# A graph convolution on one core: self loops' one-hot matrix on ScalarE, and the last four blocks prepared early and finished in a new order

## The reference

```python
h = jnp.maximum(_layernorm(x, axis=-1), 0.0)
# RGCN with mean over the neighbours of each type
out = h @ W_root + bias
for r in range(8):
    m = (edge_type == r)
    msg = h[src] @ W[r] * m[:, None]
    agg = segment_sum(msg, dst, num_segments=n)
    cnt = segment_sum(m, dst, num_segments=n)
    out = out + agg / maximum(cnt, 1.0)[:, None]
return x + out
```

## Time and profile before

| | |
|---|---|
| median of 3 runs | 1065.55 us (1061.63 to 1066.65) |
| profiled execution, its own time | 1065.97 us |
| its span, first to last instruction | 1064.2 us |
| POOL busy | 774.6 us (73%) |
| DVE busy | 800.8 us (75%) |
| PE busy | 784.8 us (74%) |
| PEld busy | 610.3 us (57%) |
| ACT busy | 273.8 us (26%) |
| mean granted TensorE clock | 0.783 of full speed |

### The profile page before, as it was taken

The page is one execution under the profiler, slowest core; times in us unless marked ns, Lnnn a source line. Parts: engine busy times, 40 slices in busy tenths (PEclk is TensorE's granted clock), DMA queues, the critical chain, the costliest instruction groups (busy, mean ns, idle before and its releaser), DMA issues.

```text
span 1064.2 us, 19429 instructions
## 1 busy us (share of the span) xinstructions
PE 784.8 (74%) x4294; PEld 610.3 (57%) x4294; DVE 800.8 (75%) x2602; ACT 273.8 (26%) x672; POOL 774.6 (73%) x821
## 2 busy tenths in 40 slices
PE   0377777777778787877878778787777877778756
PEld 0256666556566565665656556565565655656545
DVE  8799999878887766867767676776767767767674
ACT  5632222222222222222222222222222222222200
POOL 7677777777777777777777777777777777777730
PEclk9988797887877877687787877878777787777865
DMA  8594222212222222222222222222222222222210
GB/s 261 159 228 95 55 55 58 54 54 57 55 57 56 56 57 54 56 54 54 56 54 57 54 55 56 54 56 54 56 55 53 56 55 57 55 54 56 54 34 6
DMA packets 51561, 70.85 MB, mean 67 GB/s; under 512 B 13843, under 2 KB 36662, under 8 KB 51526
## 3 DMA queue, kind: packets, MB, share of 16 engines
q0 software_dynamic: 25632, 52.55, 18.9%
q1 hardware_dynamic: 25894, 17.90, 6.4%
HBM read 63.99 MB, written 6.40 MB: 66 GB/s over the span
## 4 chain that ended last, share of the span: by engine, by line
issue 37%; POOL 35%; DVE 10%; PE 7%; DMA 4%; ACT 1%; SPq 1%; POOLq 0%; DVEq 0%; ACTq 0%
POOL hg L498 35%; PE acc L1458 4%; DMA hg<-h_table,idx 4%; PE fin L1491 2%; DVE onehot L1021 2%; DVE ring L1037 2%; DVE fin L1073 1%; DVE x_all L1121 1%; DVE blk L1079 1%; DVE loophot L1026 1%; PE acc L1462 1%; SPq L402 1%; DMA x_all<-in_x 1%; PE acc L1465 0%; PE zp L1480 0%
## 5 line engine op out<-in xcount | busy, mean ns | idle before, releaser
L498 POOL DMA_INDIRECT hg<-h_table,idx x741 | 712.1, 961 | 225.8 <-issue 219.7
L1458 PE MATMUL acc<-onehot,hg 128*128 128x104 f32 (+2 forms) x1602 | 486.9, 406 | 205.0 <-DMA hg<-h_table,idx 180.3
L1458 PEld LDWEIGHTS acc<-onehot,hg 128*128 128x128 f32 x1602 | 314.5, 244 | 323.5 <-issue 202.3
L1021 DVE TENSOR_SCALAR onehot<-iota,key_f 128x104 f32<-128x104 f32 (+2 forms) x801 | 234.1, 311 | 32.2 <-DVE ring L1037 17.0
L1462 PE MATMUL acc<-onehot,ones_bf 128*128 128x104 bf16 (+2 forms) x801 | 221.9, 277 | 0.0
L610 ACT ACTIVATE idx<-src_i 128x3 int32 (+1 forms) x247 | 50.7, 205 | 542.0 <-PE acc L1465 542.0
L1037 DVE TENSOR_TENSOR ring<-ring,acc 128x512 f32 x267 | 179.9, 674 | 2.7 <-PE acc L1465 2.6
L1491 PE MATMUL fin<-w_sb,blk 128*116 128x128 f32 x864 | 159.2, 332 | 0.0
L1121 DVE SCALAR_TENSOR_TENSOR x_all<-fin,inv,x_all 116x128 f32 (+1 forms) x400 | 137.0, 342 | 15.9 <-PE fin L1491 15.4
L1491 PEld LDWEIGHTS fin<-w_sb,blk 128*116 128x116 f32 x864 | 144.6, 236 | 1.1 <-issue 0.5
L1073 DVE SCALAR_TENSOR_TENSOR fin<-ring,zp 128x464 f32<-128x464 f32 x108 | 69.6, 645 | 83.9 <-PE zp L1473 77.5
(11 more groups left out here) (135 smaller groups left out, 390.5 us busy)
## 6 DMA issues: line engine op xcount, KB each, us to landing
hg<-h_table,idx POOLq DMA_INDIRECT x741, 2.5
out<-x_all SPq DMA_DIRECT2D x53, 58.0 KB
x_all<-in_x SPq DMA_DIRECT2D x7, 384.0 KB, 6.5
h_table<-h_all SPq DMA_DIRECT2D x7, 384.0 KB
h_all<-h_table SPq DMA_DIRECT2D x5, 504.0 KB
x_all<-in_x SPq DMA_DIRECT2D x5, 504.0 KB
hg<-h_table,src_i POOLq DMA_INDIRECT x36, 5.3
w_sb<-in_L_gnn_W SPq DMA_DIRECT2D x1, 512.0 KB
```

What stands on the lines that cost most here:

```text
L498: nc.gpsimd.indirect_dma_start(out=hg[:, j, :], out_offset=None, in_=table, in_offset=bass.IndirectOffsetOnAxis(ap=idx[:, j:j + 1], axis=0 ...
L1021: nc.vector.tensor_scalar(onehot[:, t, 0:(e - a) * R].rearrange("p (r n) -> p r n", r=R), by_node[:, :, a:e], key_f[:, bass.ds(i * IT + t, ...
L1458: nc.tensor.matmul(both[:, 0, :, a:e], hg[:, slot, :], hot.rearrange("p (r n) -> p r n", r=R), start=(j == 0), stop=(j == n - 1), skip_gro ...
```

## The change

1. The comparison for `loophot` leaves VectorE. ScalarE makes the same matrix in two activations: the distance |iota - loop_key| into a new tile `loop_far`, then relu(1 - distance) into `loophot`. In iteration i and group q it does so for the following group, behind the index copy.
2. In iteration 15 TensorE transposes the own rows of blocks 50 to 53 straight from `h_all` into a free accumulator and ScalarE copies them to `tail_hT`; in iteration 16 TensorE makes their four root products with bias and VectorE adds them to `x_all` in one instruction.
3. In `end()` the four last blocks are made with a new `make_last_block`, which reads the own rows from `tail_hT` in SBUF and writes its intermediate to PSUM; the counts are transposed straight from the ring and their inverses computed from PSUM, for blocks 50 and 51 together; the products of a half start when that half of the block is there; root products, own rows and count copies are gone from there. The order of sums, blocks, additions and ring additions is new.
4. SyncE reads the flag before it waits for the stores.

```diff
                 stage(EARLY - 1, GROUPS - 1, GROUPS)
-                own(ENDB)
+                loop_onehot(EARLY + 1, 1)
                 stage(EARLY, 0, GROUPS)
-                take_counts(ENDB, slot_of(ENDB))
+                loop_onehot(EARLY + 2, 2)
                 stage(EARLY + 1, 1, GROUPS)
-                own_to_sbuf(ENDB)
-                counts_to_sbuf(ENDB)
-                for b in LASTB:
-                    own(b)
-                    own_to_sbuf(b)
-                    take_counts(b, slot_of(b))
-                    counts_to_sbuf(b)
...
+            def loop_onehot(g, q, wait_for=None):
...
+                nc.scalar.activation(loop_far[:, :], iota[0:GT * SLOTS, :], ACT.Abs,
+                                     bias=loop_key[:, bass.ds(g, 1)], scale=-1.0).then_inc(loop_far_ready, 1)
+                act.wait_ge(loop_far_ready, g + 1)
+                settled(act)
+                nc.scalar.activation(loophot[:, q, :], loop_far[:, :], ACT.Relu,
+                                     bias=ones[0:GT * SLOTS, 0:1], scale=-1.0).then_inc(loophot_ready, 1)
...
-                nc.vector.tensor_scalar(loophot[:, q, :], iota[0:GT * SLOTS, :], loop_key[:, bass.ds(g, 1)], None,
-                                        ALU.is_equal).then_inc(loophot_ready, 1)
...
+            def make_last_block(b):
...
+                for half, z_done in ((0, z_low), (1, z_high)):
+                    rs = slice(half * (R // 2), (half + 1) * (R // 2))
+                    dve.wait_ge(blk_made, 2 * b + half)
+                    nc.vector.scalar_tensor_tensor(out=tail_own, in0=ring[:, 1, rs, slot], scalar=LOOP_FLAG / 2, in1=h_b,
+                                                   op0=ALU.is_ge, op1=ALU.mult).then_inc(own_part_made, 1)
+                    dve.wait_ge(z_done, b)
+                    dve.wait_ge(own_part_made, 2 * b + half + 1)
+                    nc.vector.tensor_tensor(blk[:, rs, :], ring[:, 0, rs, slot], tail_own, ALU.add).then_inc(blk_made, 1)
...
             def end():   # VectorE
+                b0, b1, b2, b3 = TAILB
+                onehots(ENDI, 0, GT, inverse_counts(b0 - 1))
                 add_group(EARLY - 2, 3, at[0])
+                onehots(ENDI, 1, GT, add_terms(b0 - 1, range(0, 3)))
                 add_group(EARLY - 1, 4, at[1])
+                finish_sums(b0, EARLY)
                 finish_sums(b1, EARLY)
+                in_turn(add_terms(b0 - 1, range(3, ADDS)))
+                make_last_block(b0)
+                add_group(EARLY, 0, at[2], 2 * b0)
+                onehots(ENDI, 2, GT, [])
+                last_inverses(0, b0, 2)
+                add_last_terms(b0)
+                onehots(ENDI, 3, GT, [])
+                make_last_block(b1)
                 add_group(EARLY + 1, 1, at[3])
+                add_last_terms(b1)
+                onehots(ENDI, 4, GT, [])
+                add_group(EARLY + 2, 2, at[4])
...
                 add_group(EARLY + 4, 4, at_last[1])
                 finish_sums(b2, ENDG)
+                make_last_block(b2)
                 add_group(ENDG, 0, at_last[2])
+                last_inverses(1, b2, 1)
                 add_last_terms(b2)
                 add_group(ENDG + 1, 1, at_last[3])
                 finish_sums(b3, GALL)
+                make_last_block(b3)
+                last_inverses(2, b3, 1)
                 add_last_terms(b3)
...
             def end():   # TensorE
+                b0, b1, b2, b3 = TAILB
+                relations(b0 - 1, R // 2 - 1, R // 2, z_low)
+                root_of(b0 - 1)
+                relations(b0 - 1, R // 2, R, z_high)
                 sums_of(ENDI, 0, GT)
+                tail_counts(0, b0, 2)
+                last_relations(b0)
                 sums_of(ENDI, 1, GT)
                 sums_of(ENDI, 2, GT)
+                last_relations(b1)
                 sums_of(ENDI, 3, GT)
+                pe.wait_ge(tail_inv_step, 2)
                 sums_of(ENDI, 4, GT)
...
                 sums_of(ITERS - 1, 0, GT)
+                tail_counts(1, b2, 1)
+                last_relations(b2)
                 sums_of(ITERS - 1, 1, GT)
+                tail_counts(2, b3, 1)
+                last_relations(b3)
...
-            sp.wait_ge(stored, 16 * BLOCKS)
             sp.wait_ge(flag_ready, 1)
             general = sp.value_load(flag[0:1, 0:1], min_val=0, max_val=1)
+            sp.wait_ge(stored, 16 * BLOCKS)
```

More of the change, by code:

```diff
@@ L26 @@
 ENDG = (ITERS - 1) * GROUPS
-LASTB = range(BLOCKS - LAG - 1, BLOCKS)
-ENDB = LASTB[0] - 1
+TAILB = range(BLOCKS - LAG - 2, BLOCKS)
+ENDB = TAILB[0]
 ENDI = ITERS - 2
@@ L176, in rgcn @@
         hT = sb("hT", [P, BLK])
+        tail_hT = sb("tail_hT", [P, len(TAILB), BLK])
+        tail_unflag = sb("tail_unflag", [BLK, len(TAILB), R])
+        tail_cnt1 = sb("tail_cnt1", [BLK, len(TAILB), R])
+        tail_inv = sb("tail_inv", [BLK, len(TAILB), R])
         even = sb("even", [BLK, F])
@@ L672, in iteration @@
                         act.wait_ge(zeros_made, 1)
-                    g = g - 1
-                    if not isinstance(g, int) or (AHEAD - 1) * GROUPS <= g < GALL - GROUPS:
-                        stage(g, (q - 1) % GROUPS, GROUPS)
-                    elif (AHEAD - 3) * GROUPS <= g < (AHEAD - 2) * GROUPS:
-                        stage(g, (q - 1) % GROUPS, 2 * GROUPS)
+                    if not isinstance(g, int) or (AHEAD - 1) * GROUPS <= g - 1 < GALL - GROUPS:
+                        stage(g - 1, (q - 1) % GROUPS, GROUPS)
+                    elif (AHEAD - 3) * GROUPS <= g - 1 < (AHEAD - 2) * GROUPS:
+                        stage(g - 1, (q - 1) % GROUPS, 2 * GROUPS)
+                    if static(g):
+                        loop_onehot(g, q, 1)
+                    part_wait = PART_GROUPS.index(g + 1) + 1 if isinstance(g, int) and g + 1 in PART_GROUPS else None
+                    loop_onehot(g + 1, (q + 1) % GROUPS, part_wait)
                     if b is not None:
@@ L690, in iteration @@
                         words_to_sbuf(part_at(i, q, 3, 2))
+                    if static(i, STATICS - 2) and q == 2:
+                        act.wait_ge(tail_T, 1)
+                        nc.scalar.activation(tail_hT[:, :, :].rearrange("p b n -> p (b n)"), tailT,
+                                             ACT.Copy).then_inc(tail_hT_ready, 1)
                     if part_at(i, q, 3, 4) is not None:
@@ L1252, in whole_order, with add_tail_roots @@
                 nc.vector.tensor_reduce(bad1[:, :], bad[:, :], AX.X, ALU.max).then_inc(bad_ready, 1)
+            def add_tail_roots():
+                x_tail = x_all[0:BLK, TAILB[0]:, :].rearrange("p b f -> p (b f)")
+                dve.wait_ge(tail_root, 1)
+                nc.vector.tensor_tensor(x_tail, tail_roots, x_tail, ALU.add).then_inc(tail_root_added, 1)
             def parts_ready():
@@ L1483, in relations @@
             def relations(b, r0, r1, done):
-                if r0 == 0:
+                if r0 == 0 and done is None:
                     pe.wait_ge(blk_made, 2 * b + 2)
@@ L1512, in iteration @@
                         pe.wait_ge(loop_key_ready, part_at(i, q, 4, 0) + 1)
+                    if static(i, STATICS - 2) and q == 3:
+                        pe.wait_ge(tail_hT_ready, 1)
+                    if static(i, STATICS - 1) and q == 3:
+                        pe.wait_ge(tail_root_added, 1)
                     if n:
@@ L1531, in iteration @@
                             relations(b, 0, R // 2 - 1, None)
+                    if static(i, STATICS - 2) and q == 1:
+                        tail_transposes()
+                    if static(i, STATICS - 1) and q == 1:
+                        tail_products()
                     if part_at(i, q, 3, 1) is not None:
@@ L1540, in check_sum, with tail_transposes, tail_products @@
                 pe.wait_ge(loop_key_ready, len(PARTS))
+            def tail_transposes():
+                pe.wait_ge(group_added, (STATICS - 2) * GROUPS - 1)
+                for k, b in enumerate(TAILB):
+                    last = nc.tensor.transpose(tailT[:, k * BLK:(k + 1) * BLK], h_all[0:BLK, b, :], ident[0:BLK, 0:BLK])
+                last.then_inc(tail_T, 1)
+            def tail_products():
+                pe.wait_ge(group_added, (STATICS - 1) * GROUPS - 1)
+                for k, b in enumerate(TAILB):
+                    to = tail_roots[:, k * F:(k + 1) * F]
+                    nc.tensor.matmul(to, tail_hT[:, k, :], wr_sb[:, :], start=True, stop=False)
+                    last = nc.tensor.matmul(to, ones[0:1, 0:BLK], bias_sb[:, :], start=False, stop=True)
+                last.then_inc(tail_root, 1)
@@ new lines, in tail_counts, with last_relations @@
+            def tail_counts(k, b, n):
+                pe.wait_ge(summed, b + n)
+                for j in range(n):
+                    at = ((b + j) % RING) * BLK
+                    for r in range(R):
+                        last = nc.tensor.transpose(tail_cntT[k][:, j, r:r + 1], ring[0:1, 1, r, at:at + BLK], ident[0:1, 0:1])
```

(7 more changed lines are left out.)

103 lines of the change are left out of this document (51 added, 52 removed).

## The result

The changed kernel takes 1033.6 us, the median of 4 runs (1032.7 to 1034.34); the kernel before, run beside it, 1064.51 us (1061.63 to 1066.65). The ratio is 0.9707, with a 95% interval from 0.9682 to 0.9733: 31 us faster. The forecast was 1042, its range 1037.5 to 1047. The direction is right; the size is not, by 8.4 us.

A forecast was written before the change was run, and what follows sets the result against it. The kernel was taken as a queue of GpSimd gathers until the last starts, then an end of alternating VectorE and TensorE. From 1065.97 us, - 20.2 (end) - 0.8 (flag) - 2.5 (gathers) = 1042.5, so 1042; range 1037.5 to 1047.

The forecast's parts named there:

- The gathers' term: GpSimd's row gathers get shorter once the self-loop comparison leaves VectorE: 2.5 us gained, bounds 7 gained to 2 lost.
- gathers cleaned: Rival: VectorE's phases fall well in the whole loop, gathers gain the 7 us, time 1038; chance 0.07.
- the flag products: Last four blocks, both inputs now in SBUF: could cost up to 2 us of gather time; nothing was taken.
- A pair: ScalarE's two activations per group for the self-loop matrix: 0.48 us each, 1.1 us with hand-over, no cost on the path.
- the slower rival: ScalarE becomes the pace from 2.25 us a pair on; at 2.5 us a pair about 1104 us; chance 0.03.
- Iterations 15 and 16: Transposes and root products for the last blocks added there: cost 0, up to 1 us, as indices lie ready early.
- the walk: New end from 999 on: 34.1 us busy and 7.9 idle on VectorE, ending at 1041.0 instead of 1061.2, 20.2 gained.
- the rival with the lower clock: Gaps bring TensorE's lower clock earlier, half blocks cost 2.05 us each: 4.4 us more, 1046.5; chance 0.12.
- The rival of the hidden wait: A wait written by hand holds the first of the last blocks until late sums are in: 1062 to 1066; chance 0.02.
- The flag: SyncE's flag read, moved ahead of the wait for the stores: 0.8 us gained, 0 if that wait hid it.

The follow-up runs named there:

- e4: The changed kernel with an extra, unread memset of 96 x 256 bf16 per group on VectorE: 1040.46 us, ratio 0.9777.
- e5: The changed kernel with an extra, unread maximum over 96 x 256 elements into one column per group on VectorE: 1040.03 us, ratio 0.9767.
- e2: The changed kernel with the self-loop comparison back on VectorE, the other parts kept: 1047.75 us, ratio 0.9849.
- e8: The changed kernel with loads of h and x not paced after the first, and one-hots of groups 261 to 263 ahead of the waiting terms: 1032.42 us.
- e6: The changed kernel with an extra, unread comparison per group on VectorE, ahead of the group's one-hot comparisons: 1048.02 us, ratio 0.985.

## Why the prediction was right and wrong

- **What bounds the kernel.** Right: a queue of gathers up to the last one, then a chain of VectorE and TensorE. The 32.2 us split cleanly at the start of the last gather.
- **The gathers' term: the step that failed.** "Bounds: 7 us gained (half of the 14), 2 us lost; I take 2.5 gained." Measured 10.4 gained: excess 14.1 to 2.8, 11.3 us, less 0.8 of additional idle time between gathers (the hole of 1.2 at 102.9 is in it). I priced only the 28 gathers behind the self-loop comparison, 3.2 us, and took the rest of the 14 as a matter of phases that would fall as before. It isn't fixed: of the 11.3 us that went, 3.2 were the self-loop comparisons', 4.0 the one-hots' and 4.1 others', which now start elsewhere against the gathers; and e4 and e5 show 6 to 8 us come back with another instruction on VectorE that itself lengthens no gather. How much of that would fall well no row of before could tell; that nearly all did is partly luck of this order. The bound "half of the 14" came from no row; the one that nothing excluded was all 14, and with it the low end would have been 1042.5 + 2.5 - 14 = 1031 and held the time. The rival "gathers cleaned" had the mechanism and the wrong price.
- **The rule on shared interfaces was weighed on one side only.** I used what the Trainium skill's GPSIMD Engine Reference, Key points, says of two SBUF inputs against the change, and not what it says of the 2-port mode for it: the comparison that leaves VectorE, and the one-hots, are what it names. The price I gave for the flag products, up to 2 us, was a real one: they cost 0.05 us in the trace of the changed kernel, but 0.2 to 1.0 us in those of e2 to e8. That I took nothing for them came out right by luck of where they started.
- **ScalarE.** A pair is two times 0.507 us, not 0.48; from one pair's start to the next 1.25 us pass instead of 1.1, well below the 2.25 at which ScalarE would be the pace. Its wait for the block fell from 161.3 to 64.5 us, 97 us less. Cost on the path: none seen; the slower rival is dead.
- **Iterations 15 and 16.** Cost 0 as forecast; the holes in the queue of gathers are none there.
- **The new end.** The 20.9 us here against 20.2 forecast bear out the walk. Predicted from 999 on: 34.1 us busy, 7.9 idle. Measured from the point that answers to it: 34.34 busy of 40.55, so 6.2 idle. The wait for block 49's root product is 2.5 us against 3.0, that for the last sums 0.57 against 1.2, the last block's second half 0.47 against 0.9. The last group's sums start 7.65 us after its gather's start, about 5 us after the landing that I had assumed (2.6 us), as predicted. The mean granted clock was 0.81. TensorE was at the lower level in parts of the new end (8 products took 1.97 us from 1018.31 on, against 1.13 from 1016.89), but the 4.4 us of the rival with the lower clock did not come. The rival of the hidden wait is dead.
- **Missed.** The wait for x (7.6 us) and the hole of 1.2 us at 102.9. I had the slack of 1.8 us at 103.56 in hand, and asked only whether ScalarE's pairs would use it up. VectorE, faster by 0.25 us a group, ran into a load that is issued at a pace of its own.
- **The flag.** 0.8 predicted, 0.8 measured.

## What to carry to other kernels

Where GpSimd's indirect gathers are the pace, an fp32 comparison from SBUF or an instruction with two SBUF inputs on VectorE can cost them time, whatever slack VectorE has: the gather that starts while one is under way waits for its end, and the longer the instruction, the more it can cost (0.19 us for a comparison here, 0.52 for a fold). Sum the durations beyond the undisturbed one, and take that whole sum as the bound of what a change of VectorE's order can gain there; it can lose as well (e6 has 15.8 us). Moving such an instruction to ScalarE paid here although it takes ScalarE three times as long. Before a gain at one engine's pace is carried over, look at the waits on the chip it shall run on: where the index came last, most of the gain was gone.

## What was unexpected

- A gather of 0.944 us becomes 1.0 to 1.13 us when it starts during a 0.28 us comparison, and a shift of some 0.05 us makes it harmless: 64 of 64 against 3 of 45. The amount is set by when the comparison ends, to within 0.01 us.
- Over 801 gathers this sums to 14 us in one order of VectorE and 3 in another, 1.1% of the time, and the kernels e4 and e5, with extra work of 0.165 and 0.395 us per group, both take 1040 us.
- The same program takes 1064 us on some chips and 1312 on others, each with a spread of about 1%, and the change is worth 31 us on the first and, without the flag's part, 6 to 9 on the second.
